# Float16 projections, keys turned by DMA transposes, and a linear-attention state kept in float16 halves

## The reference, cut to what matters

```python
x = x + attn(layernorm(x))                # x: 8 batches x 1024 tokens x 512, float32
x = x + int8_linear(layernorm(x))

def attn(x):                              # 16 heads of 32 columns
    q, k, v = split(x @ qkv_w.T + qkv_b)
    q = relu(q) + 1e-6
    k = relu(k) + 1e-6
    kv    = cumsum(einsum('bhld,bhle->bhlde', k, v), axis=2)   # over the tokens
    k_cum = cumsum(k, axis=2)
    num = einsum('bhld,bhlde->bhle', q, kv)
    den = maximum(einsum('bhld,bhld->bhl', q, k_cum), 1e-6)
    return (num / den) @ out_w.T + out_b
```

## Time and profile before

| | |
|---|---|
| median of 3 runs | 1302.74 us (1299.88 to 1304.51) |
| the profiled execution | 1300.72 us, of which the span 1298.9 us |
| TensorE busy | 1199.1 us (92%) |
| VectorE busy | 1086.8 us (84%) |
| ScalarE busy | 568.6 us (44%) |
| GpSimd busy | 701.7 us (54%) |
| attention | about 60 to 1180 us of the span |
| linear layer | about 1180 us to the end |

### The profile page before, as it was taken

The page is one execution under the profiler, slowest core; times in us unless marked ns, Lnnn a source line. Parts: engine busy times, 40 slices in busy tenths (PEclk is TensorE's granted clock), DMA queues, the critical chain, the costliest instruction groups (busy, mean ns, idle before and its releaser), DMA issues. The chain is left out here.

```text
span 1298.9 us, 31782 instructions
## 1 busy us (share of the span) xinstructions
PE 1199.1 (92%) x10927; PEld 1058.7 (82%) x10927; DVE 1086.8 (84%) x2425; ACT 568.6 (44%) x1130; POOL 701.7 (54%) x847
## 2 busy tenths in 40 slices
PE   5789999999899999999899999999999999974998
PEld 3689888888888888898888888888898888953665
DVE  6578889888898888888888889888888898767887
ACT  4434444444344444444444444443344444422553
POOL 3355555555555555555455555555555555540887
PEclk9799999999999999999999999999999999986999
DMA  5123223222222232232222222223222231140994
GB/s 210 50 58 82 82 66 87 73 74 79 67 79 73 74 82 75 81 82 73 77 74 74 74 74 76 74 74 84 74 83 77 73 84 41 48 155 17 317 349 177
DMA packets 73950, 120.92 MB, mean 93 GB/s; under 512 B 16449, under 2 KB 16961, under 8 KB 73794
## 3 DMA queue, kind: packets, MB, share of 16 engines
q1 hardware_dynamic: 72544, 117.51, 30.6%
q10 hardware_dynamic: 1250, 1.32, 0.4%
HBM read 36.97 MB, written 31.46 MB: 53 GB/s over the span
## 5 line engine op out<-in xcount | busy, mean ns | idle before, releaser
L380 POOL TENSOR_SCALAR_AFFINE_SELECT am_hi<-am_hi 128x512 f16<-128x512 f16 x256 | 174.0, 680 | 385.4 <-DVE am_lo L826 385.4
L430 PE MATMUL unit<-xt_hi,w_hi 128*128 128x256 f32 x1024 | 306.2, 299 | 8.9 <-DVE xt_lo L801 8.0
L430 PE MATMUL unit<-xt_hi,w_lo 128*128 128x256 f32 x1024 | 292.1, 285 | 5.2 <-issue 5.2
L430 PE MATMUL unit<-xt_lo,w_hi 128*128 128x256 f32 x1024 | 291.9, 285 | 0.0
L430 PEld LDWEIGHTS unit<-xt_hi,w_hi 128*128 128x128 f32 x1024 | 197.1, 192 | 23.4 <-DVE xt_lo L801 12.9
L358 POOL TENSOR_SCALAR q_t<-q_t,eps_scaled 128x256 f32<-128x256 f32 x128 | 123.2, 962 | 147.9 <-ACT q_t L633 147.9
L430 PEld LDWEIGHTS unit<-xt_lo,w_hi 128*128 128x128 f32 x1024 | 197.3, 193 | 2.5
L430 PEld LDWEIGHTS unit<-xt_hi,w_lo 128*128 128x128 f32 x1024 | 196.9, 192 | 0.0
L633 ACT ACTIVATE q_t<-unit,qk_bias_scaled,qk_scale 128x256 f32<-128x256 f32 x128 | 72.2, 564 | 232.7 <-PE unit L430 232.7
L380 POOL TENSOR_SCALAR_AFFINE_SELECT am_lo<-am_lo 128x512 f16<-128x512 f16 x256 | 173.6, 678 | 0.0
L826 DVE SCALAR_TENSOR_TENSOR am_lo<-sc,am_hi 128x512 f16<-128x512 f32 x256 | 163.5, 679 | 9.3 <-ACT am_hi L661 9.1
(11 more groups left out here) (141 smaller groups left out, 2932.6 us busy)
## 6 DMA issues: line engine op xcount, KB each, us to landing
stack<-qk_hi SPq DMA_DIRECT2D x512, 64.0 KB, 2.0
xs<-x SPq DMA_DIRECT2D x64, 256.0 KB, 2.7
stack<-qk_lo SPq DMA_DIRECT2D x256, 64.0 KB, 2.0
out<-res SPq DMA_DIRECT2D x64, 256.0 KB, 3.3
x_spill<-xs SPq DMA_DIRECT2D x56, 256.0 KB, 2.1
w_lo<-x_spill SPq DMA_DIRECT2D x44, 256.0 KB, 4.0
w_hi<-x_spill SPq DMA_DIRECT2D x12, 256.0 KB, 4.4
stack<-qkv_wt SPq DMA_DIRECT2D x2, 768.0 KB, 7.8
```

Of the source, the lines that this page charges most:

```text
L380: ins = pool.affine_select(out=am[:, r, :, :], in_=am[:, r, :, :], compare_op=ALU.is_ge, fill=0.0, base=0, pattern=[[0, HG], [1, CHUNK]], ...
L430: mm = pe.matmul(dst[:, 0:GT], wp[:, k, f:f + P], xp[:, g % 2, k, :], start=(n == 0), stop=(n == len(terms) - 1))
```

## The change

All projections take float16 high and low parts in place of float32r, with weights and input scaled by powers of two. For this the weights' scales have to be known before the weights are split, so the order of the prologue changes, and the output weights get a bound and a scale of their own (six more small steps on VectorE). The x1 ring of the linear layer gets a buffer of its own.

Keys are no longer transposed by TensorE. `qk_hi` and `qk_lo` of the keys are turned by 16 DMA transposes a group, each of 128x128 float16, issued by SyncE between the stacking of the keys and `move_x` (`turn_keys`). The state product is three float16 matmuls for each of the four head groups in place of one float32 matmul, in reading and in writing. `keys_values` moves up to both sides of `project_out`. VectorE adds each half of the new state as one whole block of 128 partitions by 264 columns; the diagonal blocks are then split into `s_hi` (ScalarE, four pieces) and `s_lo` (VectorE, four pieces) in the next chunk. GpSimd's `add_eps` goes; the epsilon is added in both splits for the queries as it was for the keys.

```diff
-        w_hi = buf(top, "w_hi", [P, EC, 3 * E], F32R)
-        w_lo = buf(top, "w_lo", [P, EC, 3 * E], F32R)
+        w_hi = buf(top, "w_hi", [P, EC, 3 * E], F16)
+        w_lo = buf(top, "w_lo", [P, EC, 3 * E], F16)
...
-            xt_hi = buf(one, "xt_hi", [P, 2, EC, GT], F32R)
-            xt_lo = buf(one, "xt_lo", [P, 2, EC, GT], F32R)
+            xt_hi = buf(one, "xt_hi", [P, 2, EC, GT], F16)
+            xt_lo = buf(one, "xt_lo", [P, 2, EC, GT], F16)
...
+                def turn_keys(b, g, first):
+
+                    if not first:
+
+                        sp.wait_ge(st_ready, (b * (CB - 1) + GROUP * (g - 1)) * 2)
+                    for part, done, turned in ((qk_hi, qk_hi_done, kn_hi), (qk_lo, qk_lo_done, kn_lo)):
+                        sp.wait_ge(done, upto(b, GROUP * g, QK // GROUP, HG))
+                        sp.nop(nofuse=True)
+                        for j in range(GROUP):
+                            for i in range(HG):
+                                sp.dma_start_transpose(turned[:, g % 2, j, i, :], part[:, g % 2, i, j * P:(j + 1) * P]
+                                                       ).then_inc(keys_turned, 16)
+
+                sp.wait_ge(w_lo_done, 3)
                 stack_parts(0, 0, 0)
+                turn_keys(0, 0, True)
                 stack_parts(0, 0, 1)
...
                         if not (last and c // GROUP + 1 >= CB // GROUP):
                             stack_parts(b, c // GROUP + 1, c % GROUP)
+                            if c % GROUP == 0:
+                                turn_keys(b, c // GROUP + 1, first and c == 0)
                         move_x(b, c, first, last)
...
-                            if c % GROUP == 0:
-                                add_eps(b, g)
-                            else:
+                            if c % GROUP == 1:
...
-                            pe.matmul(o[:, half, i * 4 * VW:(i + 1) * 4 * VW], q_t[:, par, g, at],
-                                      state[:, g, :, :].rearrange("p h w -> p (h w)"),
-                                      start=clear, stop=False, skip_group_check=True)
-                            clear = False
+                            for qp, sp_ in ((qk_hi, s_hi), (qk_hi, s_lo), (qk_lo, s_hi)):
+                                pe.matmul(o[:, half, i * 4 * VW:(i + 1) * 4 * VW], qp[:, par, HG + g, at],
+                                          sp_[:, g, :, :].rearrange("p h w -> p (h w)"),
+                                          start=clear, stop=False, skip_group_check=True)
+                                clear = False
...
+                    if half == 0 and c % GROUP == 0:
+
+                        pe.wait_ge(keys_turned, (b * (CB // GROUP) + c // GROUP + 1) * KEY_DMAS * 16)
...
+                        if c < CB - 1:
+                            keys_values(b, c, 0, first)
                         if not (first and c == 0):
                             project_out(b, c - 1)
+                        if c < CB - 1:
+                            keys_values(b, c, 1, first)
                         projections(1)
-                        if c < CB - 1:
-                            transpose_keys(b, c, first)
...
+                def split_state(b, c):
+
+                    act.wait_ge(s_added, upto_inner(b, c, 2))
+                    if c > 0:
+
+                        act.wait_ge(s_lo_done, upto_inner(b, c - 1))
+                    for r in range(4):
+                        own = (slice(D * r, D * (r + 1)), slice(None), r, slice(None))
+                        ins = act.activation(s_hi[own], state[own], ACT.Copy)
+                    ins.then_inc(s_hi_done, 1)
...
-                        if i < HG:
-                            dve.scalar_tensor_tensor(out=qk_lo[:, i, :], in0=k_t[:, g % 2, i, :], scalar=eps_scaled[:, 1:2],
-                                                     in1=qk_hi[:, i, :], op0=ALU.add, op1=ALU.subtract).then_inc(qk_lo_done, 1)
-                        else:
-                            dve.tensor_tensor(qk_lo[:, i, :], q_t[:, g % 2, i - HG, :], qk_hi[:, i, :], ALU.subtract
-                                              ).then_inc(qk_lo_done, 1)
+                        dve.scalar_tensor_tensor(out=qk_lo[:, g % 2, i, :], in0=f_t[:, i, :],
+                                                 scalar=eps_scaled[:, 1 - i // HG:2 - i // HG], in1=qk_hi[:, g % 2, i, :],
+                                                 op0=ALU.add, op1=ALU.subtract).then_inc(qk_lo_done, 1)
...
-                    for r in range(4):
-                        own = state[D * r:D * (r + 1), 2 * half:2 * half + 2, r, :]
-                        new = st[D * r:D * (r + 1), 0:8 * VW].rearrange("p (g h w) -> p g h w", g=2, h=4)[:, :, r, :]
-                        if c == 0:
-                            ins = dve.tensor_copy(own, new)
-                        else:
-                            ins = dve.tensor_tensor(own, new, own, ALU.add)
-                    ins.then_inc(s_updated, 1)
+                        dve.wait_ge(s_added, upto_inner(b, c - 1, 2, half + 1))
+                        dve.wait_ge(s_lo_done, upto_inner(b, c - 1))
+                    own = state[:, 2 * half:2 * half + 2, :, :].rearrange("p g h w -> p (g h w)")
+                    new = st[:, 0:8 * VW]
...
+                        ins = dve.scalar_tensor_tensor(out=own, in0=new, scalar=SCORE_FACTOR, in1=own, op0=ALU.mult, op1=ALU.add)
+                    ins.then_inc(s_added, 1)
+
+                def split_state(b, c):
+
+                    dve.wait_ge(s_hi_done, upto_inner(b, c))
                     for r in range(4):
+                        own = (slice(D * r, D * (r + 1)), slice(None), r, slice(None))
+                        ins = dve.tensor_tensor(s_lo[own], state[own], s_hi[own], ALU.subtract)
+                    ins.then_inc(s_lo_done, 1)
```

More of the change, by code:

```diff
@@ L61, in build @@
     STACK_DMAS = 3 * 4
+    KEY_DMAS = 2 * GROUP * HG
     LN_STEPS = 5
[L63 to L66, removed]
+    WEIGHT_STEPS = 6
+    FEATURE_STEPS = 9
+    POWER_STEPS = 14
+    OUT_STEPS = 6
+    X_TOP = 2.0 ** 4
+    W_TOP = 2.0 ** 10
+    QK_TOP = X_TOP * W_TOP
+    WV_TOP = 2.0 ** 5
+    V_TOP = X_TOP * WV_TOP
+    V_ONE = 2.0 ** 9
+    AT_TOP = 2.0 ** 14
+    OUT_TOP = 2.0 ** 10
     SCORE_TOP = 2.0 ** 13
@@ L271, in _ @@
                 for i in range(EC):
-                    sp.dma_start(stage[i], qkv_wt[i * P:(i + 1) * P, :]).then_inc(w_loaded[i], 16)
+                    sp.dma_start(stage[:, i, :], qkv_wt[i * P:(i + 1) * P, :]).then_inc(w_loaded[i], 16)
+                sp.dma_start(wo_stage, out_wt.rearrange("(c p) n -> p c n", p=P)).then_inc(wo_loaded, 16)
                 for c in range(2, CB):
                     load_x(c)
[L275 to L281, removed]
                 def store_x1(b, c):
@@ L351, in _ @@
                     add_bias(0, c)
-                def add_eps(b, g):
-                    for i in range(HG):
-                        pool.wait_ge(qk_done, upto(b, GROUP * g, QK // GROUP, HG + i + 1))
-                        pool.nop(nofuse=True)
-                        pool.tensor_scalar(q_t[:, g % 2, i, :], q_t[:, g % 2, i, :], eps_scaled[:, 0:1], None, ALU.add
-                                           ).then_inc(q_eps_done, 1)
                 def split_values(b, c):
@@ L468, in transpose_attn @@
                     pe.wait_ge(attn_ready, upto(b, c, 2))
-                    if c % CB < CB - 1:
-                        pe.wait_ge(kn_copied, upto_inner(b, c))
+                    if not (isinstance(b, int) and b * CB + c == 0):
+                        pe.wait_ge(x1_ready, upto(b, c - 1))
                     for i in range(EC):
@@ L483, in project_out @@
                     mm.then_inc(op_ready, 1)
-                def transpose_keys(b, c, first):
-                    par, at = place(c)
-                    if not (first and c == 0):
-                        pe.wait_ge(x1_ready, upto(b, c - 1))
-                    for g in range(HG):
-                        mm = pe.transpose(misc[:, g * P:(g + 1) * P], k_t[:, par, g, at], ident[:, :])
-                    mm.then_inc(kn_ready, 1)
                 def outputs(b, c, half, first):
@@ L548, in _ @@
                     rows = P if i > 0 else 1
-                    slot = (i - 1) % 2 if i > 0 else 2
+                    term = squares[:, (i - 1) % 2, :] if i > 0 else bias_squares
                     for n, dst in enumerate(sum_banks):
-                        mm = pe.matmul(dst, ones_bf[0:rows, :], squares[0:rows, slot, n * E:(n + 1) * E],
+                        mm = pe.matmul(dst, ones_bf[0:rows, :], term[0:rows, n * E:(n + 1) * E],
                                        start=(i == 0), stop=(i == EC), skip_group_check=True)
                     mm.then_inc(sums_ready, 1)
-                pe.wait_ge(w_lo_done, EC)
+                pe.wait_ge(wo_squared, 1)
+                for k in range(EC):
```

(6 more changed lines are left out.)

228 lines of the change are left out of this document (133 added, 95 removed).

## The result

The changed kernel takes 1794.7 us (median of 4 executions, 1792.6 to 1800.1), the kernel before 1302.7 on the same chip. The ratio is 1.379, 95% interval 1.375 to 1.383. The forecast of 1450 had the direction right and the size wrong, and its range, which ended at 1620, did not hold the time. The profiled execution took 1800.1 us, its span is 1798.3.

What follows compares the result with a forecast made beforehand. SyncE's DMA list was to bound the attention, at 39.7 us a group against 35.0: 1300.7 + 8 - 1.5 + 31 x (39.7 - 35.0) = 1453, given as 1450 us, range 1250 to 1620.

Steps and rivals of the forecast that it cites:

- t: Time SyncE needs to issue one DMA transpose, shown by no row; taken as 0.59 us, like a stacking DMA.
- 28.3 + 16 t: Least period of a group in us: SyncE's chain through key stacking, x and query stacking, plus 16 transpose issues.
- the 2 us for the clock: Per group, TensorE's clock falls after its pause, slowing the work behind the first scores; up to 4, 2 taken.
- dear issue: Rival: a transpose costs SyncE over a microsecond or holds up the rings; 1882 us by the 1.56 row, chance 0.14.
- the +8: Prologue: later weight splitting and the first 16 transposes ahead of query stacking add 8 us, bounds 3 and 15.
- the forecast's own chain: On SyncE: scores, key stacking, transposes, store and load of x, query stacking, landing, next scores; period 39.7 with the clock.
- store, landing and the load behind it: Piece of SyncE's chain between key and query stacking, moving x: 2.6 us a group.
- TensorE's own saving: Cheaper 16-bit matmuls and no key transposes in the attention: 3.2 us less a group, 33.4 to 30.2.
- the term of +0.2 a group: VectorE's query splits, taking the key splits' instruction, cost 0.2 us more a group; 0 and 1.2 kept as bounds.
- The split of the state: VectorE's 224 pieces of 132 columns at 0.29 us each, 65 us in all.
- The floor of 32 without transposes: Pace of a group if nothing else bound: VectorE's 31.2 us plus 1 us lost between engines.
- the 1 us that the two lose on each other: Per group, time TensorE and VectorE lose on each other, added to VectorE's 31.2 to give a pace of 32.

Runs made afterwards that it cites:

- run 1: Changed kernel with only the 8 DMA transposes a group of the keys' high parts, the low part not turned: 1471.2 us, period 40.4.
- run 3: Changed kernel with the store and load of x issued ahead of the 16 transposes, all work kept: 1787.8 us, period 50.3.
- run 6: Kernel before with 16 DMA transposes a group of a constant tile added, into a buffer nobody reads: 1803.9 us, period 51.0.
- run 2: Changed kernel without DMA transposes in the loop, the keys turned in the prologue used in all groups: 1287.2 us, period 34.2.
- run 11: Changed kernel, TensorE turning the next chunk's keys early, state added in eight diagonal pieces, split by ScalarE and GpSimd, all work kept: 1225.1 us, ratio 0.942.
- run 8: Changed kernel without transposes in the loop and without VectorE's split of the state, s_hi read for s_lo: 1226.2 us, period 32.1.
- run 7: Changed kernel with TensorE turning the float16 keys and keys_values back in its old place, all work kept: 1316.5 us, ratio 1.013.
- run 10: Changed kernel, TensorE turning keys, keys_values in its old place, state added in diagonal pieces and split by ScalarE and GpSimd: 1282.9 us, ratio 0.987.
- run 4: Changed kernel with the 16 transposes moved to the odd chunk, behind the query stacking, all work kept: 1727.3 us, period 48.1.
- run 5: Changed kernel with each of the 16 transposes turning 64 feature rows instead of 128: 1790.0 us.

## Why the prediction was wrong, point by point

**The step that failed: the size of t.** The period was written as 28.3 + 16 t, with t unknown and bounded by 0.35 and 1.56. I took 0.59, "the row nearest in kind". Measured is 1.28. With it the formula gives 28.3 + 20.4 = 48.7, with the 2 us for the clock 50.7, and the sum 1300.7 + 8 - 1.5 + 31 x (50.7 - 35.0) = 1794; the period was 50.6 and the profiled execution took 1800.1. The mechanism and the place held (runs 1, 3 and 6), one term was half of what it should have been, and it is multiplied by 16 x 31: 0.69 too little is 342 us, all but a few of what was missing. The rival "dear issue" was the right case, at a chance of 0.14. The upper end of the range stopped at t = 0.85, though the bound was 1.56; nothing in the trace excluded what lay between.

**What is luck in 1794.** The first key stacking in the loop comes 14 us later than the +8 allows, and the loop with its end is 8 shorter than 31 x 15.7 - 1.5. The 28.3 also counts 0.6 too much: the landing of 2.0 in the earlier trace rows runs from the start of an issue, and was added behind its end. And the 50.7 is the sum of the forecast's own chain, while in the group shown that chain takes 6.9 + 8.6 + 20.4 + 2.7 + 9.5 = 48.1 (the last from 780.65 to the landing at 790.14), and the other one fills the 2.3 up to the scores.

**The Trainium skill on this.** "DMA: Bandwidth & Descriptors" (the table on instruction decode) gave 0.73 or more as an estimate; its 631 cycles are for a transpose from HBM to SBUF, and here it is SBUF to SBUF. Measured is 1.28: the direction agrees, the size is far short. "Advanced Engine Details and Errata" (X-Bar Transpose) has transposes as fast as regular DMAs. For the issue on SyncE that does not hold here: 1233 ns against 590 for a copy from SBUF to SBUF in the same kernel; the landing, 2.4 against 2.0, is near.

**A wait not followed.** The formula took the load of x as off the path: "store, landing and the load behind it". It is the landing of this load that VectorE's statistics wait for, and TensorE behind them, and in three groups of four this ends last. Run 3 shows that it was worth 0.3 us a group: without it the forecast's chain, with the lower clock in it, is nearly as long. It cost next to nothing in the sum, but what the trace was to show, scores waiting for a stacking DMA once a group, is put down so in only 6 cases (28.3 us), not 31.

**The clock: the size near, the place not.** 2 us a group were set down, in the 6.9 behind the scores. In the group shown these 6.9 are as long as before. TensorE works at half clock ahead of the scores, between 785.12 and 789.7, 4.6 us for 2.3, in the chain of the load. The windows agree (0.54 and 0.61), and the mean clock from 400 to 700 is 0.81. In run 3 the half clock falls where the forecast had it, and there it costs 1.4 (8.3 in place of 6.9).

**TensorE's own saving: as computed, and of no use there.** Float16 matmuls of 512 columns are 0.216 apart, of 256 columns 0.11, of 132 some 0.057. In run 2 TensorE's work is 266/300 x 34.2 = 30.3 a group, where 30.2 was forecast. What this is worth in time no run shows by itself: run 11 keeps all work and is faster than the kernel before, but it also has another order and handles the state otherwise, and these were not tried on the kernel before alone.

**VectorE: one term right, two wrong.** The groups of the kernel after:

```profile
L858 DVE SCALAR_TENSOR_TENSOR qk_lo<-f_t,eps_scaled,qk_hi 128x256 f16<-128x256 f32 x256 | 156.9, 654 | 55.0 <-ACT qk_hi L675 53.3
...
L939 DVE TENSOR_TENSOR s_lo<-state,s_hi 32x132 f16<-32x132 f32 x224 | 108.6, 485 | 8.1 <-ACT s_hi L700 2.3
...
L931 DVE SCALAR_TENSOR_TENSOR state<-st,state 128x264 f32<-128x264 f32 x96 | 41.1, 428 | 5.8 <-PE st L559 5.8
```

The block add was forecast at 0.425 and takes 0.428. The query splits did not become dearer. Both kinds together take 654 ns on average, where 860 and 566 make 713, and the query splits alone (the last four of the eight of a group) 0.483 where they took 0.566: the term of +0.2 a group was a gain of 0.3. In run 11, where the engines have less time to spare, they take 0.58. The split of the state was forecast at 0.29 and takes 0.485, 44 us more. Four of them together take 1.98 us just while GpSimd works through its masks; the second row has the durations of all (min/median/max):

```profile
796.08 1.98 DVE L939 TENSOR_TENSOR s_lo<-state,s_hi 32x132 f16<-32x132 f32 x4
```

```profile
L939 DVE TENSOR_TENSOR s_lo<-state,s_hi x224: 284/390/779, 102.0 to 1663.6; 32x132 f16<-32x132 f32 x112
```

The 91 of them with no GpSimd instruction beside them take 0.284 to 0.294, just the forecast's 0.29; the 133 beside one take 0.62 on average. So the size was right and the waiting was left out. The block add, which reads the new values from PSUM, takes 0.43 beside GpSimd too.

The rule that the prediction cites from the Trainium skill ("SBUF — State Buffer") agrees with this: two inputs in SBUF on VectorE, and a GpSimd instruction that reads SBUF at the same time. I had applied it to the query splits and not to these.

**The floor of 32 without transposes: too low.** Run 2 shows 34.2 in its place. The engines' work was as forecast: VectorE's is 273/300 x 34.2 = 31.1, where 31.2 was set down. What was mis-sized is the 1 us that the two lose on each other, which is 3.1. Taking VectorE's state splits away gives back 2.1 (run 8). Order counts as much: in run 7 both engines are some 87% busy and the period is 35.75, and between runs 10 and 11 the order alone makes some 1.6.

**Prologue: +22 where +8 was set down and 15 was the bound.** The first key stacking comes at 45.69 in place of 36.18, 9.5 later and not 4, and 16 transposes take 20.4 in place of 9.4. The bound had been worked out with t = 0.59, not with the upper end of t.

## What to carry to other kernels

An instruction that only issues a DMA still costs its queue time. Sixteen of them on a list that is part of the critical loop are sixteen times the price on the path, whether or not anyone waits for their data (run 6). When a price is not in the trace and the formula multiplies it by hundreds, the range has to go to both bounds of the price. And after a wait has been found, go down each engine's list behind it and look for the second one: here two chains of nearly the same length lay side by side (run 3), and moving the transposes closed a third (run 4).

## What was not expected of the hardware

- A DMA transpose of 128x128 in 16 bits from SBUF to SBUF occupies SyncE for 1.23 us at the median and 1.28 on average with gaps, against 0.59 for a copy. With 64 rows in place of 128 it is the same 1.23 (run 5).
- TensorE turns eight 128x128 float16 tiles in 0.44 us (two starts of four in run 11, 714.81 and 715.03, and the next matmul at 715.25), as long as four float32 tiles took before (596.87 - 596.44). Sixteen DMA transposes took 20.4 us for the same tiles of two chunks.
- One GpSimd subtraction of 128x528 takes 1.18 us and the four VectorE pieces of 32x132 that it replaces 1.94 on average (4 x 0.485), at a quarter of the elements. Without GpSimd beside them the four would take 1.17 (4 x 0.292).
